# Transposes moved to the head of their own step in two cross-attention layers, maxima spread between the projections in the first

## The reference

```python
q, k, v = norm(x) @ Wq, ctx @ Wk, ctx @ Wv      # per head
p = softmax(q @ k.T / sqrt(d))                   # over 4096 context rows
x = x + (p @ v) @ Wo + bo
```

## Time and profile before

| | |
|---|---|
| three runs | 1929.84, 1932.38, 1934.37 us; median 1932.38 |
| profiled execution | 1927.47 us, its span 1925.5 us |
| TensorE, matmuls | 1664.0 us busy, 86% |
| VectorE | 1117.2 us, 58% |
| ScalarE | 793.3 us, 41% |
| GpSimd | 499.8 us, 26% |
| TensorE's clock, mean | 0.913 of full speed |
| layer 0 | from the start to about 640 us |
| layer 1 | from about 1040 to 1740 us |

### The profile page before, as it was taken

How to read it: one execution, slowest core, us unless ns; L and a number is a source line. 1 busy time by engine, 2 the same in 40 slices (tenths; PEclk the granted TensorE clock), 3 DMA queues, 4 the chain that set the end, 5 groups by cost and what they waited for, 6 DMA issues and landing times. The chain is left out here.

```text
span 1925.5 us, 26912 instructions
## 1 busy us (share of the span) xinstructions
PE 1664.0 (86%) x10311; PEld 1208.0 (63%) x10311; DVE 1117.2 (58%) x1880; ACT 793.3 (41%) x1084; POOL 499.8 (26%) x630
## 2 busy tenths in 40 slices
PE   5889999999999668779997888999999899885289
PEld 3667777777777467568886555555566555342278
DVE  4766666666653465356654777776756777106651
ACT  3435554554544132224442111555556455661110
POOL 0003433433469000000000200443433434640000
PEclk9989999999999877679998777899999999997589
DMA  2112221222222100022230110111001010000243
GB/s 77 44 44 67 66 61 50 67 67 58 53 60 52 33 1 1 23 88 87 87 98 11 33 32 27 31 34 34 23 23 34 23 34 12 2 1 22 88 156 117
DMA packets 75443, 92.35 MB, mean 48 GB/s; under 512 B 7442, under 2 KB 62276, under 8 KB 75332
## 3 DMA queue, kind: packets, MB, share of 16 engines
q1 hardware_dynamic: 75140, 90.79, 15.8%
q10 hardware_dynamic: 192, 0.05, 0.0%
HBM read 73.47 MB, written 0.52 MB: 38 GB/s over the span
## 5 line engine op out<-in xcount | busy, mean ns | idle before, releaser
L571 POOL CAST st<-ef 32x512 fp32r<-32x512 f32 x384 | 233.0, 607 | 397.9 <-PE score L1136 354.4
L1676 DVE TENSOR_REDUCE mx<-bank 128x1 f32<-128x512 f32 x512 | 311.8, 679 | 42.2 <-PE bank L1148 41.6
L757 ACT ACTIVATE P<-score 128x1024 f32<-128x1024 f32 x256 | 255.9, 1025 | 129.1 <-PE score L1136 128.8
L1148 PE MATMUL bank<-ef,qm 128*128 128x512 f32 x512 | 234.4, 505 | 41.3 <-DVE mx L1676 21.4
L948 PE MATMUL bank<-c_hi,w_split 128*128 128x512 f32 x640 | 233.1, 425 | 23.7 <-DVE c_lo L1542 8.4
L1148 PEld LDWEIGHTS bank<-ef,qm 128*128 128x128 f32 x512 | 105.9, 207 | 154.9 <-DVE mx L1676 107.4
L1136 PE MATMUL score<-qs,st 97*128 97x512 f32 x512 | 173.3, 426 | 12.9 <-ACT P L757 8.7
L948 PEld LDWEIGHTS bank<-c_hi,w_split 128*128 128x128 f32 x640 | 128.7, 201 | 78.1 <-issue 39.8
L1567 DVE TENSOR_REDUCE mx<-bank 128x1 f32<-128x512 f32 x256 | 162.3, 682 | 22.1 <-PE bank L993 13.6
L536 POOL TENSOR_TENSOR sum<-sum,P 128x512 f32<-128x512 f32 x84 | 111.2, 1324 | 210.0 <-ACT P L673 210.0
L673 ACT ACTIVATE P<-score 128x1024 f32<-128x1024 f32 x128 | 129.9, 1024 | 78.5 <-PE score L982 76.0
(11 more groups left out here) (315 smaller groups left out, 2646.0 us busy)
## 6 DMA issues: line engine op xcount, KB each, us to landing
c_in<-in_ctx SPq DMA_DIRECT2D x64, 512.0 KB, 4.0
w<-k SPq DMA_DIRECT2D x128, 128.0 KB, 2.2
arena<-in_L_ffn_w SPq DMA_DIRECT2D x16, 1024.0 KB, 5.2
arena<-in_L_ffn_W SPq DMA_DIRECT2D x16, 1024.0 KB, 5.4
x<-in_x SPq DMA_DIRECT2D x1, 512.0 KB, 3.7
raw<-in_L_xattn_Wk SPq DMA_DIRECT2D x1, 512.0 KB, 6.4
raw<-in_L_xattn_Wv SPq DMA_DIRECT2D x1, 512.0 KB, 7.3
raw<-in_L_xattn_Wq SPq DMA_DIRECT2D x1, 512.0 KB, 8.1
```

The costliest lines, as they stand in the source:

```text
L571: pool.tensor_copy(st1[32 * block:32 * block + 32, k, :], ef1[rows, g % LAG, part, :].bitcast(F32)).then_inc(a[f"st{k}"], 16)
L757: act.activation(P1[:, index % PRING, :], score[n % 2][:], ACT.Exp).then_inc(a["p"], 1)
L1148: mm(dst[:], qm1[:, h, 128 * q:128 * q + 128], ef1[:, g % LAG, 0, :], start=True, stop=True).then_inc(a["ms"], 1)
L1676: v.tensor_reduce(mx1[:, u % 2, i, n:n + 1], ring[n % 3][:], AX.X, ALU.max).then_inc(a["red"], 1)
```

## The change

The transposes of chunk t move from the end of step t-1 to the head of step t, in both layers, with `c_hi` and `c_lo` on ScalarE and VectorE. In layer 0 the projection of keys 0 moves from behind the eight maxima to between maxima 3 and 4; its copy on ScalarE comes after the third exponential, its low part on VectorE after reduction 5. The order of users of the ring is now a list per layer, `order0` and `order1`, from which both the bank and the wait are computed. In layer 1 the sum of the denominators moves behind the first pair of scores, with its copy on ScalarE behind the first exponential, and values 0 behind the transposition of the shift row. The buffer `ef1` gets ten slots instead of nine, and the buffers behind it move.

```diff
+ERING = LAG + 1
-        ef1 = at("ef1", 0, [LAG, 2, CHUNK], F32R)
+        ef1 = at("ef1", 0, [ERING, 2, CHUNK], F32R)
...
+        order0 = ["d", "t0", "t1", "m0", "m1", "m2", "m3", "k0", "m4", "m5", "m6", "m7", "k1", "v0", "v1"]
+        order1 = ["t0", "t1", *(f"m{n}" for n in range(16)), "k0", "v0", "v1"]
+        def use0(t, use):
+            kind, n = use[0], int(use[1:] or 0)
+            if kind == "d":
+                return ("dc", (t - LAG) // NCH) if t > LAG and (t - LAG) % NCH == 0 else None
+            if kind == "m":
+                return ("red", 8 * (t - 1) + n + 1) if 1 <= t <= CHUNKS else None
+            return ({"t": "cl", "k": "kl", "v": "v"}[kind], 2 * t + n + 1) if 0 <= t < CHUNKS else None
...
+        def freed(a, t, use):
+            order, used = (order0, use0) if a is a0 else (order1, use1)
+            place = order.index(use) - 3
+            while True:
+                if place < 0:
+                    t -= 1
+                    if t < 0:
+                        return None
+                    place += len(order)
+                before_it = used(t, order[place])
+                if before_it:
+                    return before_it
+                place -= 3
```

ScalarE, layer 0:

```diff
-                    if g >= 0:
-                        for h in range(HPU0):
+                    if 0 < t < CHUNKS:
+                        for f in range(2):
+                            context_high(a, c_hi0, t, f)
+                    for h in range(HPU0):
+                        if g >= 0:
                             weights(g, h)
+                        if h == 2 and t < CHUNKS:
+                            keys(t, 0)
                     if t < CHUNKS:
-                        for n in range(2):
-                            keys(t, n)
+                        keys(t, 1)
...
-                    if t + 1 < CHUNKS:
-                        for f in range(2):
-                            context_high(a, c_hi0, 13 + f, t + 1, f)
```

TensorE, layer 0:

```diff
+                    if 0 < t < CHUNKS:
+                        turn(a, t, 0)
+                        turn(a, t, 1)
                     for h in range(HPU0):
                         if g >= 0:
                             scores(g, h)
                         if 1 <= t <= CHUNKS:
                             maxima(t - 1, h)
+                        if h == 1 and t < CHUNKS:
+                            keys(t, 0)
                     if g >= 0:
                         mixture(g, 0)
                     if t < CHUNKS:
-                        keys(t, 0)
                         keys(t, 1)
...
-                    if t + 1 < CHUNKS:
-                        turn(a, freed0, 13, t + 1, 0)
-                        turn(a, freed0, 13, t + 1, 1)
```

VectorE, layer 0:

```diff
+                    if 0 < t < CHUNKS:
+                        context_of(t)
+                    for h in range(HPU0):
+                        if 1 <= t <= CHUNKS:
                             reduce(t - 1, h)
+                        if h == 2 and t < CHUNKS:
+                            low_keys(t, 0)
```

TensorE, layer 1:

```diff
+                    if 0 < t < CHUNKS:
+                        turn(a, t, 0)
+                        turn(a, t, 1)
                     for n in range(8):
                         if g >= 0:
                             if n == 1 and g and g % NCH == 0:
+                                sums(g // NCH - 1)
                                 pe.wait_ge(a["dc"], a.n("dc", g // NCH))
                             scores(g, n)
```

More of the change, by code:

```diff
@@ new lines, in bank_of @@
+        def bank_of(a, t, use):
+            return ring[order0.index(use) % 3] if a is a0 else ring[(order1.index(use) + 1) % 3]
+        def freed(a, t, use):
[11 more added lines that the diff above has]
+                place -= 3
@@ L726, in cross0 @@
                     if t < CHUNKS:
-                        for n in range(2):
-                            values(t, n)
-                    if t + 1 < CHUNKS:
-                        for f in range(2):
-                            context_high(a, c_hi0, 13 + f, t + 1, f)
+                        values(t, 0)
+                        values(t, 1)
                     if t % NCH in (2, 3, 4, 5) and t // NCH + 1 < UNITS:
@@ L794, in cross1 @@
                     u, i = divmod(t, NCH)
-                    if g > 0 and g % NCH == 0:
-                        sums(g // NCH - 1)
-                    if g >= 0:
-                        for n in range(8):
+                    if 0 < t < CHUNKS:
+                        for f in range(2):
+                            context_high(a, c_hi, t, f)
+                    for n in range(8):
+                        if g >= 0:
+                            if n == 1 and g and g % NCH == 0:
+                                sums(g // NCH - 1)
                             weights(g, n)
@@ L803, in cross1 @@
                         mixed(g // NCH)
-                    if t < CHUNKS and u % 2 == 0:
-                        values(u, i, 0)
                     if i == 0 and 0 < t <= CHUNKS:
@@ L808, in cross1 @@
                     if t < CHUNKS and u % 2 == 0:
+                        values(u, i, 0)
                         values(u, i, 1)
-                    if t + 1 < CHUNKS:
-                        for f in range(2):
-                            context_high(a, c_hi, 19 + f, t + 1, f)
                 sums(UNITS - 1)
@@ L1221, in cross1 @@
                         mixture(g, 1)
-                    if t < CHUNKS and u % 2 == 0:
-                        values(t, 0)
                     if i == 0 and 0 < t <= CHUNKS:
@@ L1713, in cross1 @@
                         v.tensor_copy(wout1[:], score[1][:].rearrange("p (k n) -> p k n", k=4)).then_inc(set1["wop"], 1)
-                    if 1 <= t <= CHUNKS:
-                        for h in range(HPU1):
+                    if 0 < t < CHUNKS:
+                        for f in range(2):
+                            context_low(a, c_hi, c_lo, t, f)
+                    for h in range(HPU1):
+                        if 1 <= t <= CHUNKS:
                             reduce(t - 1, h)
@@ L1722, in cross1 @@
                         finish(g // NCH - 1)
-                    if t + 1 < CHUNKS:
-                        for f in range(2):
-                            context_low(a, c_hi, c_lo, 19, t + 1, f)
                     if i == 0 and 0 < t < CHUNKS:
```

149 lines of the change are left out of this document (59 added, 90 removed).

## The result

**Slower by 5.7%.** Four runs of the changed kernel have a median of 2039.84 us (2038.99 to 2044.63), four of the kernel before beside them 1931.11 (1928.92 to 1934.37): ratio 1.0567, 95% interval 1.0543 to 1.059. The forecast was 2028, with a range of 1979 to 2052. The profiled execution took 2038.99 us, its span is 2037.3, TensorE's mean clock 0.89.

The account below looks back on a forecast made before the run. The prediction took TensorE's own stream to set the pitch of layer 0's steady steps. Its terms, 59.8 + 27.6 + 21.6 + 5 - 13 = +101.0 on 1927.47, gave 2028 us, range 1979 to 2052.

Parts of the forecast that it names:

- Part 1: Layer 0, steps 9 to 31: new TensorE waits, mainly before maximum 6, +2.6 us a step, +59.8 us.
- the old one of 0.79 goes: Layer 0's steady steps: the first two maxima's 0.79 us wait for banks the context's low parts leave would disappear.
- Part 2: Layer 0, steps 9 to 31: clock falls in 0.8 of 23 steps, 1.5 us each, +27.6 us.
- Part 3: Layer 0 before the first scores: steps 2 to 8 at 16.3 us against 13.22, +21.6 us; step 1, +5 us.
- Part 4: Layer 1: low queries hidden in VectorE's wait for ScalarE, 1.02 us in 14 of 16 steps; layer's sum -13 us.
- About +2 against -2: Layer 1: denominators' sum behind the first exponential and query masks before the low context, about +2 us against -2.
- The clock holds: Rival: Part 2 and the clock share of Part 3 go; +57.8 us, 1985 us; chance 0.18.
- Faster: the bank is free in time: Rival, layer 0: the chain to the low keys ends before scores 3, no stall at maximum 6; 1901 us; chance 0.05.
- Two stretches a step: Rival, layer 0's 23 steps: clock falls for two stretches a step, 2050 to 2065 us; chance 0.10.

Follow-up runs that it names:

- experiment 3: Changed kernel with 32 products of zeros ahead of maximum 6 in layer 0's steps with scores, except each unit's first: 2015.81 us, ratio 1.0403.
- experiment 2: Changed kernel with copies of keys 0 before the third exponential on ScalarE: 2024.93 us; second kernel, also low keys 0 before reductions 4 and 5: 1982.2 us.
- experiment 5: Changed kernel with products of zeros behind each pair of maxima in layer 0's steps 2 to 8: 2026.08 us, ratio 1.0504.
- experiment 8: Kernel before with layer 1's change, plus four products of zeros behind each pair of maxima in its steps 2 to 8: 1915.13 us, ratio 0.9913.
- experiment 4: Changed kernel with layer 0's keys 0 one pair of maxima later, behind maximum 5, on TensorE alone: 1958.75 us, ratio 1.013.
- experiment 7: Kernel before with layer 1's whole change, nothing of layer 0's: 1922.94 us; then the same with the sums left ahead of all scores: 1914.83 us.
- experiments 7 and 9: The latter: kernel before with layer 1's change, sums left, zero products in its steps 2 to 8: 1908.18 us; also in layer 0's: 1902.39 us.

## Why the prediction was right, point by point

**Part 1, the new waits, +59.8: size right, layout incomplete.** By the 0.44 of experiment 3, 28.6 us of the 488.0 are clock, and so are 1.5 of the 400.4 before; 459.4 - 398.9 leaves 60.5 for the waits. The wait at maximum 6, from the end of scores 3, is 2.36 us in the ordinary step and was forecast at 2.60; the stalls at the transposes and at keys 0 are 0.47 and 0.11, forecast at 0.58 and 0.24. But an ordinary step is 20.14, 3.1 above 17.05, not 2.6; steps without copies of queries are 19.4 at the full clock (in the trace of experiment 3), 2.35 above. The step of the forecast that failed is "the old one of 0.79 goes": scores 0 to scores 1 are 447.73 to 449.88, 2.15 us, where they were 2.21. Maximum 1 still waits for the context's low part (449.54), since the copies of the queries now stand ahead of its high part on ScalarE; in the step at 512.08, which has none ahead of it, the wait is indeed gone. The whole trace agrees: from scores 0 to scores 1 are 2.15 us in each of the eight steps with copies at their head (11 to 14 and 19 to 22), and 1.51 to 1.56 in 13 of the other 15. So 0.73 of the 0.79 stays in eight of the 23 steps. I counted every instruction that the transposes take along and missed one that they are moved behind. That the sum fits all the same is in part luck: against 2.6 a step the eight ordinary steps give 4 us more, and the steps without copies and those around the units' ends give about as much less.

**Part 2, the clock, +27.6: right in cause and size, by another count.** 28.6 us against 27.6; experiment 3 took most of it away by filling the wait, and experiment 2 all of it by shortening the wait. The forecast counted 18.4 steps with one short stretch at half clock each. There were 15, four of them with a double one, which makes 19. The rule of the Trainium skill (TensorE: Matmul & The Clock Gate, "HAM oscillation — how this bites in real kernels") that I read strictly as leaving such waits alone does not hold in that reading: waits of 2.2 to 2.4 us went with 64.9 us at half clock, and with products in them 13.7 were left. The same page, in "A second HAM failure mode: psum-queue depth-cycling", tells of another kernel in which frequent short idle moments between groups of matmuls make the clock go to and fro; the row of steps 9 to 31 at 0.93 agrees with that.

**Part 3, layer 0 before the scores, +21.6 and +5: mechanism right.** The steps came to 15.8 us, forecast 16.3. At the full clock they were forecast at 14.1; they are 13.7 without copies of queries and 14.6 in step 8, and 14.1 to 15.0 with the products of experiment 5. Step 1 cost 8.3 instead of 5, with 10.2 us at half clock in it that I had not put in.

**Part 4, layer 1, -13: the mechanism of the low queries right, the sum wrong.** From the stretch before its step 2 to its last steps the layer came out at -3.8. The steps with low queries are 16.2 instead of 17.2, as forecast, but only behind step 8; and of the -12.9 some is clock (20.5 us at half clock became 10.2). In steps 2 to 8, four of which have the wait, the gain of some 4 us shows as 0.2. More half clock hides it: 71.7 us instead of 54.6. With the clock held the stretch is 107.1 us (experiment 8). If a us at half clock costs 0.16 in the kernel before too, its 118.1 would be 109.4 with the clock held, and the change gains 2.3 there (an estimate; the kernel before was not run with products in this stretch). That the shorter waits bring the additional half clock is not shown: the traces of experiments 4 and 5, with the same code in layer 1, have 58.0 us of it and take 116.1 us. "About +2 against -2" for the sums and the masks was wrong too: the sums cost 2.8 us in two steps at the full clock, and up to 6.6 with the half clock beside them (experiment 7). The +4.1 before step 2 is not shown to be the change's: kernels with the same code there (experiments 7 and 9, sums left) read 462.8 and 466.0 in that stretch, with 150.2 and 160.4 us at half clock.

**The sum.** The trace has 10.8 us more than the +101.0. The forecast was short by 3.3 in step 1, 2.8 before layer 1's step 2, 1.2 in layer 1's steps 2 to 31, 5.2 in its last steps and 1.8 behind them, and 3.7 too high in layer 0's steps 2 to 8. The steady steps of layer 0 fit within 0.2.

**The rivals.** "The clock holds" falls with 64.9 us at half clock. "Faster: the bank is free in time" named the right condition: experiment 4 does away with the wait, and in steps 9 to 31 it is the equal of the kernel before. It is not faster as a whole, since its steps 2 to 8 are the longest of all. "Two stretches a step" happened in four steps of the 23.

**What stays open.** Why a step of 20.14 us keeps the full clock at one time and, with the same gaps, not at another; how much of the 5.2 us in layer 1's last steps is the sums and how much chance; and what makes the half clock in layer 1's steps 2 to 8 differ (58.0 to 71.7 us) between traces of the same code.

## What to carry to other kernels

- When a user of a rotating set of buffers is moved, look up who takes its buffer next, and lay out the whole chain up to that point through the program order of every engine in it. One pair of maxima later (experiment 4) was worth 87 us in the steady steps.
- When an operation moves to the head of a step, list on each engine what stood behind it in the old step: that now stands ahead of it.
- A gain on an engine with gaps can vanish in TensorE's clock. Where TensorE idles again and again by tenths of a microsecond, products of zeros into an unused bank in those gaps are worth a test; they gave 10.4 us in one stretch and 6.4 in another. They are not always free: in experiment 5 they cost about 0.4 us a step.

## What the runs showed of the hardware

- Idle time that TensorE is given to fill changes its clock and the length of the stretch: 117.5 us at 0.72 against 107.1 at 1.00, with 224 matmuls more, 0.22 us each and overlapping in the pipeline.
- Waits need not be long. Each of layer 1's steps 3 to 7 in the changed kernel has one gap of 0.65 us before a maximum and otherwise gaps of about 0.1, and the clock over steps 2 to 8 is 0.70; steps of layer 0 with one gap of 2.2 to 2.4 us keep 1.00 in some cases and lose it in others, and the second kernel of experiment 2, with 0.33 us where that gap was, keeps it in all 23.
- What a us at half clock costs depends on how much of the stretch TensorE sets: 0.44 us in layer 0's steady steps (22.6 of 51.2), 0.16 in layer 1's steps 2 to 8 (10.4 of 64.9).
- The same instructions can have more or less half clock. Layer 1's steps 2 to 8, with the same code, have 58.0 us of it and take 116.1 us in the traces of experiments 4 and 5, and have 71.7 and take 117.9 in the changed kernel's. So a difference of ten us at half clock between two traces of such a stretch does not show what the change did.
